# A transformer block on one core: batch 1's first layer norm turned by VectorE and DMA instead of TensorE, with an earlier loading order

## What is computed

```python
mod = (silu(c) @ wmod)            # six sections of 512: sa, ca, ga, sb, cb, gb
h = layernorm(x) * (1 + ca) + sa  # per batch
q, k, v = h @ Wqkv + bqkv         # 128 wide each, one head
x = x + ga * (softmax(q k^T / sqrt(128)) v @ Wo + bo)
h = layernorm(x) * (1 + cb) + sb
x = x + gb * (h @ W_up^T + lora of the expert that gate_w chooses)
```

## Time and profile before

| | us |
|---|---|
| median of 3 runs | 183.2 |
| the profiled execution, its own time | 182.96 |
| its span, first to last instruction | 181.2 |
| TensorE busy | 170.8 (94%) |
| VectorE busy | 139.6 (77%) |
| ScalarE busy | 90.1 (50%) |
| GpSimd busy | 80.4 (44%) |

### The profile page before, as it was taken

The page is one execution under the profiler, slowest core; times in us unless marked ns, Lnnn a source line. Parts: engine busy times, 40 slices in busy tenths (PEclk is TensorE's granted clock), DMA queues, the critical chain, the costliest instruction groups (busy, mean ns, idle before and its releaser), DMA issues.

```text
span 181.2 us, 2841 instructions
## 1 busy us (share of the span) xinstructions
PE 170.8 (94%) x924; PEld 134.9 (74%) x924; DVE 139.6 (77%) x352; ACT 90.1 (50%) x170; POOL 80.4 (44%) x109
## 2 busy tenths in 40 slices
PE   6867999999999999999999999999999999999990
PEld 5845655978758778878687777788887878768890
DVE  3647759998888988978999929699388285988965
ACT  3347124975167895139349562713487512483100
POOL 3374200179452719240988960017695000362650
PEclk9999999999999999999999999999999999999999
DMA  3999998851014002344020763001140000001415
GB/s 130 313 352 379 387 385 234 269 206 52 0 54 183 0 0 50 98 109 157 0 114 33 213 139 83 0 0 56 65 149 26 0 2 0 0 4 58 174 41 190
DMA packets 13918, 21.32 MB, mean 118 GB/s; under 512 B 3356, under 2 KB 4128, under 8 KB 13904
## 3 DMA queue, kind: packets, MB, share of 16 engines
q1 hardware_dynamic: 13904, 21.15, 35.1%
HBM read 14.83 MB, written 4.21 MB: 105 GB/s over the span
## 4 chain that ended last, share of the span: by engine, by line
PE 57%; DVE 18%; ACT 8%; SPq 6%; DMA 6%; issue 4%; POOL 0%; DVEq 0%; ACTq 0%; POOLq 0%
PE bank L400 37%; SPq L322 5%; DMA stage<-in_L_wmod_dram 4%; PE bank L414 3%; DVE xs L1236 3%; ACT xn_p L849 3%; DVE stats L1243 3%; DVE xn L1169 2%; PE bank L524 2%; DVE f_gb L1301 1%; DVE h1lo L1158 1%; DVE h2lo L1174 1%; PE bank L509 1%; PE bank L503 1%; DMA stage<-xn 1%
## 5 line engine op out<-in xcount | busy, mean ns | idle before, releaser
L400 PE MATMUL bank<-wup_lo,h2hi 128*128 128x512 f32 (+1 forms) x68 | 27.2, 401 | 0.4 <-ACT h2hi L907 0.4
L400 PE MATMUL bank<-wup_hi,h2hi 128*128 128x512 f32 (+1 forms) x68 | 26.0, 382 | 0.0
L888 ACT ACTIVATE xn_p<-xs,shift,rstd 128x512 f32<-128x512 f32 x16 | 13.1, 816 | 25.9 <-POOL shift L1498 25.8
L400 PE MATMUL bank<-wup_hi,h2lo 128*128 128x512 f32 (+1 forms) x68 | 25.9, 381 | 0.0
L1495 POOL TENSOR_TENSOR rstd<-var_eps,neg_half 128x1 f32<-128x1 f32 x16 | 8.9, 554 | 37.2 <-DVE var_eps L1247 37.2
L1510 POOL TENSOR_TENSOR xs<-xs,f_gb 128x512 f32<-128x512 f32 x14 | 17.9, 1292 | 7.7 <-DVE f_gb L1301 7.7
L400 PE MATMUL bank<-h1lo,wqkv_hi 128*128 128x512 f32 x48 | 19.7, 411 | 1.6 <-ACT wqkv_hi L881 1.2
L1487 POOL TENSOR_TENSOR xs<-xs,gabo 128x512 f32<-128x512 f32 x16 | 20.3, 1308 | 0.1
L400 PE MATMUL bank<-h1hi,wqkv_hi 128*128 128x512 f32 x48 | 19.0, 395 | 0.0
L400 PE MATMUL bank<-h1hi,wqkv_lo 128*128 128x512 f32 x48 | 18.9, 394 | 0.0
L1219 DVE TENSOR_TENSOR plo<-bank,phi 128x512 fp32r<-128x512 f32 x16 | 10.0, 684 | 6.7 <-ACT phi L857 6.6
(11 more groups left out here) (185 smaller groups left out, 410.0 us busy)
## 6 DMA issues: line engine op xcount, KB each, us to landing
out_dram<-xs SPq DMA_DIRECT2D x15, 256.0 KB, 2.0
stage<-in_L_wmod_dram SPq DMA_DIRECT2D x3, 1024.0 KB, 8.0
xs<-in_L_wmod_dram SPq DMA_DIRECT2D x3, 1024.0 KB, 7.6
xs<-in_L_attn_x_dram SPq DMA_DIRECT2D x3, 1024.0 KB, 8.4
stage<-xn SPq DMA_DIRECT2D x32, 64.0 KB, 2.0
f_gb<-in_L_ffn_W_up_dram SPq DMA_DIRECT2D x1, 1024.0 KB, 11.4
gb_bc<-gates_dram SPq DMA_DIRECT2D x4, 256.0 KB, 4.1
xn_p<-in_L_attn_Wqkv_dram SPq DMA_DIRECT2D x4, 192.0 KB, 6.5
```

What stands on the lines that cost most here:

```text
L400: mm = nc.tensor.matmul(dst, w, m, start=first and i == 0, stop=last and i == total - 1)
L888: nc.scalar.activation(xn2_p[:, t, :], xs[:, b, t, :], ACT.Identity, bias=shift[:, 1, t:t + 1], scale=rstd[:, 1, t:t + 1]).then_inc(S["xn2 ...
```

## The change

- **Loads.** Batch 0's x comes in two DMAs of two tiles instead of 1, 1 and 2 tiles, with no wait of SP between the first loads; sb and cb go to `f_gb`, `W_up` to the place of batch 2's x, so that sb is not waited for and batch 2's x is loaded later, after `w_up_transposes`.
- **First tiles.** On TensorE tile 1 of batch 0 is turned ahead of `modulation(0)`, and the columns of ca are turned between tiles 2 and 3.
- **ga.** `first_gate_everywhere` uses transposes in place of matmuls.
- **Batch 1** is turned by VectorE and DMA (`TURNED` = 1); `x1_transposes` is gone. `w_up_transposes` stands in its place on TensorE, `modulation(3)` ahead of `out_projection(0)`.
- **VectorE's order.** The four `turn_blocks(1)` stand between the steps of batch 0's qkv; `ln1_stats(2, (0, 1))` is moved behind the residuals; `wup_low` and `h1_low(1)` change places, and each `h1_low(1, t)` alternates with `residual(0, t)` and `ln2_moments(0, t)`.
- **Gate product.** In the loops of batches 1 and 2 `gate_ffn(b - 1, 0)` stands between `residual(b, 0)` and `ln2_moments(b, 0)`; the others keep their places.

```diff
-TURNED = 2
+TURNED = 1
...
-        (2, "x1T", 1, 0), (4, "x1T", 1, 1), (6, "x1T", 1, 2), (7, "x1T", 1, 3), (5, "O", 0),
+        (5, "O", 0),
...
-        raw = {"ca": stage[:], "sa": xs[:, 2], "ga": xs[:, 3], "sb": stage[:], "cb": stage[:], "gb": xs[:, 3],
-               "wup": f_gb, "wqkv": xn2_p}
+        raw = {"ca": stage[:], "sa": xs[:, 2], "ga": xs[:, 3], "sb": f_gb[:], "cb": f_gb[:], "gb": xs[:, 3],
+               "wup": xs[:, 2], "wqkv": xn2_p}
...
-            for i, ts in enumerate((slice(0, 1), slice(1, 2), slice(2, 4))):
-                sp.dma_start(xs[:, 0, ts], x_v[0, :, ts, :]).then_inc(x0_in[i], 16)
+            for i in range(2):
+                sp.dma_start(xs[:, 0, 2 * i:2 * i + 2], x_v[0, :, 2 * i:2 * i + 2, :]).then_inc(x0_in[i], 16)
             load_section("ca")
-            sp.wait_ge(x0_in[1], 16)
             load_wqkv((0, 1))
-            sp.wait_ge(x0_in[2], 16)
             load_section("sa")
...
             load_section("ga")
-            wait_used(0)
             load_section("sb")
-            wait_used(1)
-            sp.dma_start(xs[:, 2], x_v[2]).then_inc(x_in[2], 16)
             sp.dma_start(wo_raw[:], wo).then_inc(wo_in, 16)
             sp.dma_start(bo_bc[:], bo.partition_broadcast(P)).then_inc(bo_in, 16)
-            sp.dma_start(raw["wup"][:], wup.rearrange("(o p) h -> p o h", p=P)).then_inc(wup_in, 16)
+            wait_used(1)
+            sp.dma_start(raw["wup"], wup.rearrange("(o p) h -> p o h", p=P)).then_inc(wup_in, 16)
...
             load_section("cb")
             load_section("gb")
+            move_turned(1)
+            sp.wait_ge(S["wupT_psum"], NK)
+            sp.dma_start(xs[:, 2], x_v[2]).then_inc(x_in[2], 16)
             write_gate(0)
             spread_gate(0, 1)
...
-                    mm = nc.tensor.matmul(dst[:, kt * P:(kt + 1) * P], gate_col[:, 0, kt, 0:1].to_broadcast([P, P]), ident[:],
-                                          start=True, stop=True)
+                    mm = nc.tensor.transpose(dst[:, kt * P:(kt + 1) * P], gate_col[:, 0, kt, 0:1].to_broadcast([P, P]), ident[:])
...
+            first_x1_transposes((1,))
             modulation(0)
-            first_x1_transposes((1,))
-            keep_warm(bank[5], 1)
             first_x1_transposes((2,))
+            first_modulation_columns(0)
             first_x1_transposes((3,))
-            first_modulation_columns(0)
             first_modulation_columns(1)
...
-            x1_transposes(1)
+            w_up_transposes(range(NK))
             pv(0)
-            w_up_transposes(range(NK))
-            qkv(1, (0,))
+            modulation(3)
             out_projection(0)
-            qkv(1, (1,))
-            modulation(3)
+            qkv(1, (0, 1))
             gate_transposes()
+            qkv(1, (2,))
             lora_b_transposes()
-            qkv(1, (2,))
             modulation_columns(3)
...
-            h1_high(1, (0, 1))
+            wup_high((0, 1))
             wo_high(0)
-            h1_high(1, (2, 3))
+            wup_high((2, 3))
             o_high(0)
-            wup_high(range(NK))
+            h1_high(1)
+            modulation_rows(3)
             ln2_normalise(0, (0, 1))
-            modulation_rows(3)
...
-                    nc.vector.tensor_scalar(xn1[:, t, :], xs[:, 1, t, :], moments[:, 0, t, 0:1], rstd[:, 0, t:t + 1],
+                    nc.vector.tensor_scalar(xn1_blocks[:, :, :, t].rearrange("p a k i -> p k a i"),
+                                            xs[:, 1, t, :].rearrange("p (k a i) -> p k a i", k=NK, a=NB),
+                                            moments[:, 0, t, 0:1], rstd[:, 0, t:t + 1],
                                             ALU.subtract, ALU.mult).then_inc(S["xn1_ready"], 1)
...
             qkv_shift_row()
+            turn_blocks(1, (0,))
             qkv_shift()
+            turn_blocks(1, (1, 2))
             qk_low(0)
-            ln1_stats(2, (0, 1))
+            turn_blocks(1, (3,))
             maxima(0)
...
-            h1_low(1)
+            wup_low(range(NK))
             split_sb()
             inverse_sums(0)
             o_low(0)
-            wup_low(range(NK))
             for t in range(NT):
+                h1_low(1, (t,))
                 residual(0, t)
                 ln2_moments(0, t)
...
+            ln1_stats(2, (0, 1))
             add_parts("cb")
...
                         residual(b, t)
+                        if t == 0:
+                            gate_ffn(b - 1, 0)
                         ln2_moments(b, t)
-                        if t != 1:
-                            gate_ffn(b - 1, (0, 0, 1, 2)[t])
+                        if t >= 2:
+                            gate_ffn(b - 1, t - 1)
```

More of the change, by code:

```diff
@@ L198, in adaln_block @@
         wqkv_in = [sem(f"wqkv_in{kt}") for kt in range(NK)]
-        x0_in = [sem(f"x0_in{i}") for i in range(3)]
+        x0_in = [sem(f"x0_in{i}") for i in range(2)]
         x_in = [sem(f"x_in{b}") for b in range(B)]
@@ L473, in first_x1_transposes @@
                             mm.then_inc(S["x1T_psum"], 1)
-            def x1_transposes(b):
-                xn1_done(pe, b)
-                for kt in range(NK):
-                    dst = open_bank("x1T", b, kt)
-                    for t in range(NT):
-                        mm = nc.tensor.transpose(dst[:, t * P:(t + 1) * P], xn1[:, t, kt * P:(kt + 1) * P], ident[:])
-                    mm.then_inc(S["x1T_psum"], 1)
             def qkv(b, kts, js=range(3)):
@@ L1019, in ln1_stats @@
                     if b == 0:
-                        dve.wait_ge(x0_in[min(t, 2)], 16)
+                        dve.wait_ge(x0_in[t // 2], 16)
                     else:
@@ L1164, in h1_low, with turn_blocks @@
                                                    ALU.subtract).then_inc(S["h1_lo"], 1)
-            def turn_blocks(b):
-                for t in range(NT):
+            def turn_blocks(b, tiles=range(NT)):
+                for t in tiles:
                     xn1_done(dve, b, t + 1)
```

## The result

| us | kernel before | changed kernel |
|---|---|---|
| median (20 runs each) | 182.79 | 183.75 |
| lowest, highest | 182.27, 186.09 | 182.93, 185.30 |
| the profiled execution, its own time | 182.96 | 184.47 |
| its span | 181.2 | 182.7 |

The ratio of the times is 1.0062, with an interval of 1.0042 to 1.0082: the change makes the kernel about 1 us slower. The forecast was 182.6 us, a little faster. The profiled execution after lies 0.72 us above its median, the one before 0.17 above, so the two traces differ by more (1.5 us) than the kernels do.

The account below looks back on a forecast made before the run. VectorE's list up to batch 1's first row maximum was taken as the bound, TensorE from 99 to 152 us being fixed. Gains of 0.4 and 0.2 us turn 182.96 into 182.4, with the median offset 182.6 us; range 181.6 to 184.3.

Parts of the forecast that it names:

- The step on the tiles: Start, behind modulation 0: fewer TensorE steps let ScalarE's first high part start at about 13.0 instead of 13.88, 0.85 us.
- rival 2: At the start ca and x land 0.6 us earlier: 182.0 us; against: batch 1's x ties first maximum; chance 0.23.
- Blocks and transposes: VectorE before batch 0's first maximum: blocked normalisation takes 0.48 us a tile, and four block transposes of 0.65 fit gaps.
- P V and the first residual: TensorE's second part: P V starts at 37.42 and the first residual at 43.1 instead of 45.95, seemingly 2.8 us won.
- the one on the moves: SP's 16 moves of batch 1, 0.63 us each: last starts at 39.0, lands at 41.0, hidden before the residual.
- 0.6 us of cover: Margin between batch 1's first high and low parts, done at 42.5, and the first residual at 43.1.
- Rival 1: SP between gb and batch 2's x: moves come late, delaying the residual; 184.0 us, at the bound 184.7; chance 0.22.
- its deciding point: Last move of batch 1 landing after 41.6 us; each us beyond costs one.
- VectorE's list: From first residual to batch 1's first maximum: VectorE's longer work takes the gain back, ending at 61.15 instead of 61.57.
- the good case: At batch 1's first maximum, with the moves hidden: a gain of only 0.4 us.
- The gate product: VectorE between residual and moments: fills the wait for the residual's result, saving 0.2 us for batch 1, nothing for batch 2.
- Sum: End of kernel: 0.4 at batch 1's first maximum plus 0.2 makes 0.6 us, 182.96 to 182.4; forecast 182.6 us.

Follow-up runs that it names:

- experiments 7: Changed kernel with each residual of batch 0 and its moments put ahead of the low part of batch 1's h1; 184.41 us.
- experiment 8: Changed kernel without the 16 moves of batch 1 and with GpSimd's output bias addition to batch 0's x cut to 2 columns; 182.58 us.
- experiment 2: Kernel before with first tiles, ga, gate product, all new loads and batch 2's statistics behind the residuals; batch 1 still turned by TensorE; 182.16 us.
- 1 and 9: Kernel before with, in 1, the first tiles, ga and gate product alone, 181.93 us; in 9, the first loads besides, 181.80 us.
- experiment 6: Changed kernel with cb loaded early: in the first kernel ahead of the small loads, 184.33 us; in the second behind them, 183.20 us.

## Why the prediction was wrong, step by step

**The start.** The step on the tiles was right. ScalarE's first high part starts 2.38 us after modulation 0's first matmul (10.86, shown above), where it was 3.29: 0.91 us less, for a forecast of 0.85. ca landed 0.27 us later in this execution, so the row shows 13.24 instead of 13.0.

```profile
13.24 1.27 ACT L794 ACTIVATE h1hi<-bank,modT_ca 128x512 fp32r<-128x512 f32 x2 [0.83 <-PE bank L469]
...
18.36 2.47 DVE L1011 BATCH_NORM_STATS2 stats<-xs 128x6 f32<-128x512 f32 x4 [0.35 <-DMA xs<-in_L_attn_x_dram]
```

How much of it reaches the first maximum is another matter. In the two traces that moves by only 0.34 us, and it comes 11.33 us after VectorE's first statistic of batch 1 (18.36), where it was 11.62. The ten variants have 11.31 to 11.43 (one 11.94, where VectorE did not wait for batch 1's x), while that statistic starts anywhere between 16.44 and 18.11 us. So the first maximum follows the landing of batch 1's x, as rival 2 says against itself, and the order of the tiles gives it about 0.3 us. From the medians the first maximum stands at 182.79 - 121.39 - 31.54 = 29.86 before and 183.75 - 121.18 - 33.60 = 28.97 after, 0.9 us earlier; but that is a remainder, and no trace shows where the other 0.6 comes from. That it meets the forecast of 0.85 is in part luck.

**Blocks and transposes.** The blocked normalisation takes 1.92 us, 0.48 a tile, as taken. The Trainium skill (VectorE: DVE Perf Modes, What auto-detection actually checks) lets an operation with a single source keep its faster mode if source and destination are in SBUF and their outermost sizes are even, and the trace agrees. The four block transposes of 0.65 to 0.70 fit ahead of the first maximum, where VectorE even idles 0.70 us.

**P V and the first residual.** The output projection allowed the residual 14.1 us after M0 (experiments 7 and 8, where it released the residual); the step had 13.9. Right.

**The step that failed** is the one on the moves: "The last move starts at 39.0 and lands at 41.0 ... hidden, with 0.6 us of cover". The time of the issue was right (last at 39.4, and SP was even 0.2 us earlier against M0), but not its reason: the prediction took it from one load less in the queue, while SP, through with its small loads at 26.93, waited for modulation 2. The landing was priced by a row of batch 2, 2.02 us, where the queue held nothing else; here the moves stood behind 2 MB that had been issued 0.5 us before, and ScalarE could start only 3.4 us after the last issue: the last landing was some 13.1 us behind M0 instead of 11.8. And "A high and a low part of 0.7 each" priced the low part by the earlier trace rows, beside which GpSimd stood idle: it took 1.59. Together 1.3 + 0.85, less the 0.6 of cover, is 1.5 us, the cell of the table. Rival 1 had the place and the sign, and named the DMA engines that the moves share with cb and gb, but priced only a late SP. Against M0 the last landing ran 0.7 us past its deciding point (41.6 - 29.18 = 12.4), which it priced at 0.7; the other 0.8 is the long low part, which no rival had.

**VectorE's list** was right: 18.17 us from residual to maximum for 18.05. It was also the reason why even the good case promised only 0.4 us, and experiment 8 shows that this was optimistic by 0.6: the stretch is 32.6, not 32.0, with the moves and the additions away, since among other things VectorE waits 0.49 us for the lora weights, which the sum had ready just in time.

**The gate product** was to give 0.2 us. In the trace the second residual of batch 1 starts 2.28 us after the first, where it was 2.49: the 0.2 us are there. Whether they reach the end is not shown: from the first maximum of batch 1 to the end the changed kernel has 0.21 less, the other kernels with the same exchange 121.17 to 121.48 (121.39 before): no more than 0.1 can be made out.

**Sum.** The stretch loses 2.06 us: 0.6 for the statistics (experiment 2), 1.3 for the first residual behind its 14.1, 0.2 for the rest of turning batch 1 (net of the 1.8 us by which the output projection now allows the first residual sooner). The end gains 0.2 in the two traces, and the start what the medians then leave, 0.9. The forecast had the stretch at 0.4 lost.

## What to carry to other kernels

Take a transfer's time from issue to landing out of a row with the same queue in front of it, not from a quiet one: 2.0 us became 5.0 in the median behind 2 MB of loads, at nearly the same cost of issue. When a step is moved from one memory to another, look at which engine reads the new place at that moment: two engines that never met before may now wait for each other. And a change of several parts deserves a run of each: here the small parts alone (1 and 9) are 0.5 to 0.9% faster than before, and the large one takes it all back.

## What the runs showed of the hardware

**GpSimd and VectorE in SBUF.** The contention goes both ways (0.74 to 1.59 and 1.72 us for the low part beside additions, 0.55 to 0.98 for a deviation, an instruction of one column, beside a low part).

**A full queue holds the issuing engine.** SP's issue of a 1 MB load takes 0.37 us at 28.82, with little in the queue, and 2.07 to 2.71 us at 7 to 12 us, behind several MB; the 256 KB of `wo` at 12.22 are held as long (the rows of SP's queue above). In experiment 6, with another 1 MB in front of them, the small loads held SP for 10.9 us instead of 8.1, and so made the moves behind them late.

**TensorE's clock.** In the profiled executions of five variants TensorE, after it had stood idle some 1.6 us in front of batch 1's scores, was granted 0.50 of its speed (1.2 instead of 2.4 GHz) for 3 to 4 us, and its products took 0.63 us instead of 0.40. Three more (in the table "changed", "changed, cb behind the small loads" and "changed, neither") idled 1.6 us there too and kept the full clock. With the residual first (columns as above):

```profile
56.00:58.00 2.00, 2.00 (x19) 1.91 (x17) 1.90 (x6) 1.98 (x4) 0.00 (x0) 1.00 0.01 4
58.00:60.00 2.00, 0.42 (x3) 0.11 (x2) 1.97 (x11) 1.43 (x3) 1.02 (x1) 1.00 0.00 0
...
62.00:64.00 2.00, 2.00 (x7) 1.41 (x6) 1.97 (x5) 0.04 (x1) 1.47 (x2) 0.50 0.04 8
```

It cost little, since VectorE's list ends last there: from the first maximum of batch 1 to the end the five take 121.34 to 121.41 us and the three with the full clock 121.17 to 121.29, so 0.2 us at most; the kernel before has 121.39.

**Left open.** In the second kernel of experiment 6 the last moves, issued at 37.2 and 37.8, still landed 2.5 to 3.2 us after their issue, though the DMA engines showed a share of only 0.45, 0.28 and 0.07 in the three us from 38 on. What held them there was not tried.
